# A transformer block on one core: halves of the attention output copied and added by GpSimd, q and k projected earlier

## The reference

```
def attention(x):                       # 16 heads of 64, batch 2, T = 1024
    q, k, v = x @ Wq, x @ Wk, x @ Wv
    logits = (q @ k^T + causal + position bias) / 64
    return softmax(logits) @ v @ Wo + bo
def moe(x):                             # one shared expert, 8 routed, top 2
    h = gelu(x @ Wfc + bfc) @ Wproj + bproj      # for each expert
    return shared + sum(gate_e * h_e)
x = x + norm(attention(norm(x)))
x = x + norm(moe(norm(x)))
```

## Time and profile before

| | |
|---|---|
| median of 3 runs | 946.14 us (944.57 to 946.49) |
| the profiled execution | 943.02 us, span 941.2 us |
| busy share of the span | TensorE 83%, VectorE 74%, ScalarE 67%, GpSimd 40% |
| TensorE's mean granted clock | 0.958 |
| attention, heads 0 to 15 | about 51 to 691 us |
| one turn of the loop (323.4 to 399.4 us) | 76.0 us, TensorE busy 66.9, VectorE 56.9, ScalarE 56.5, GpSimd 30.6 |

### The profile page before, as it was taken

The page is one execution under the profiler, slowest core; times in us unless marked ns, Lnnn a source line. Parts: engine busy times, 40 slices in busy tenths (PEclk is TensorE's granted clock), DMA queues, the critical chain, the costliest instruction groups (busy, mean ns, idle before and its releaser), DMA issues.

```text
span 941.2 us, 17424 instructions
## 1 busy us (share of the span) xinstructions
PE 784.5 (83%) x4244; PEld 640.4 (68%) x4244; DVE 700.9 (74%) x1564; ACT 632.4 (67%) x1404; POOL 377.5 (40%) x419
## 2 busy tenths in 40 slices
PE   3757799889888889879988988898657999999993
PEld 2546677668677778767767777777436777777772
DVE  5455587678778677858777867876658888889886
ACT  3356677767767776867777777786346677777763
POOL 1448544334435244324433433441231244444422
PEclk9998899999999999999999999999967999999997
DMA  7752433343344334433334334432100311111101
GB/s 249 264 170 64 96 74 79 81 95 84 68 95 99 76 67 90 95 79 73 81 90 97 69 79 102 84 72 63 56 23 1 115 68 67 67 67 67 45 1 45
DMA packets 61691, 79.01 MB, mean 84 GB/s; under 512 B 37312, under 2 KB 46656, under 8 KB 58304
## 3 DMA queue, kind: packets, MB, share of 16 engines
q1 hardware_dynamic: 61344, 77.84, 32.4%
q10 hardware_dynamic: 288, 0.59, 0.3%
HBM read 35.22 MB, written 9.63 MB: 48 GB/s over the span
## 4 chain that ended last, share of the span: by engine, by line
PE 47%; issue 15%; DVE 13%; DMA 10%; POOL 8%; ACT 4%; SPq 2%; DVEq 1%; POOLq 0%; ACTq 0%
PE out_ps L1298 11%; PE trans_ps L1280 8%; PE score_ps L1256 7%; DMA k_hl<-k_hl 5%; PE shared_ps L1312 3%; DMA inv_scratch<-normed 3%; PE score_ps L1168 2%; PE trans_ps L1168 2%; PE score_ps L1170 2%; PE score_ps L1169 2%; PE trans_ps L1169 2%; PE trans_ps L1170 2%; DVE pT_lo L949 2%; DVE pT_lo L1055 2%; POOL k_hl L544 2%
## 5 line engine op out<-in xcount | busy, mean ns | idle before, releaser
L936 DVE CUSTOM_DVE_ANT_0 score_ps<-score_ps,bias 128x128 f32<-128x128 f32 (+7 forms) x256 | 195.0, 762 | 117.7 <-PE score_ps L1256 96.1
L755 ACT ACTIVATE pT_hi<-trans_ps 128x512 fp32r<-128x512 f32 (+3 forms) x384 | 185.4, 483 | 124.6 <-PE trans_ps L1280 115.3
L1256 PE MATMUL score_ps<-k_hl,q_hl 128*128 128x512 f32 (+2 forms) x768 | 192.0, 360 | 40.9 <-DMA k_hl<-k_hl 32.3
L1280 PE MATMUL trans_ps<-ident,probs 128*128 128x128 f32 x1152 | 195.8, 282 | 35.0 <-DVE pT_lo L949 32.7
L949 DVE TENSOR_TENSOR pT_lo<-trans_ps,pT_hi 128x512 fp32r<-128x512 f32 (+3 forms) x384 | 204.2, 553 | 27.6 <-ACT pT_hi L755 25.7
L730 ACT ACTIVATE probs<-score_ps,row_min 128x128 f32<-128x128 f32 (+7 forms) x256 | 187.9, 734 | 35.2 <-DVE row_min L936 33.5
L1280 PEld LDWEIGHTS trans_ps<-ident,probs 128*128 128x128 f32 x1152 | 139.2, 144 | 74.0 <-DVE pT_lo L949 44.3
L1256 PEld LDWEIGHTS score_ps<-k_hl,q_hl 128*128 128x128 f32 x768 | 134.3, 191 | 71.4 <-ACT probs L730 26.8
L1298 PE MATMUL out_ps<-pT_hi,v_hl 128*128 128x512 f32 (+2 forms) x384 | 152.4, 401 | 17.9 <-DVE o_pair L967 17.9
L1055 DVE TENSOR_TENSOR pT_lo<-probs,pT_hi 128x512 fp32r<-128x512 f32 x144 | 133.7, 956 | 24.8 <-ACT pT_hi L824 14.3
L831 ACT ACTIVATE probs<-score_ps,layer_bias_T 128x512 f32<-128x512 f32 x144 | 98.5, 686 | 56.2 <-PE score_ps L1170 53.5
(11 more groups left out here) (127 smaller groups left out, 1249.2 us busy)
## 6 DMA issues: line engine op xcount, KB each, us to landing
q_hl<-k_hl SPq DMA_DIRECT2D x64, 256.0 KB, 3.3
k_hl<-k_hl SPq DMA_DIRECT2D x32, 512.0 KB, 4.3
v_scratch<-probs SPq DMA_DIRECT2D x16, 512.0 KB, 4.0
v_raw<-v_scratch SPq DMA_DIRECT2D x32, 256.0 KB, 3.9
inv_all<-inv_scratch SPq DMA_DIRECT2D x64, 128.0 KB, 3.1
bias_all<-gate_scratch SPq DMA_DIRECT2D x8, 1024.0 KB, 4.5
v_raw<-in_Wfc SPq DMA_DIRECT2D x8, 256.0 KB, 4.8
bias<-in_Wproj SPq DMA_DIRECT2D x8, 256.0 KB, 5.2
```

The source lines that it names most:

```text
L755: act.activation(pT_hi[c][:, CH * g:CH * g + m, q * P:(q + 1) * P], trans_ps[k % 2][:, 0:m * P].rearrange("p (m q) -> p m q", q=P), ACT.Co ...
L936: dve.tensor_tensor_reduce(out=ps, in0=ps, in1=bias_b[b][:, T - n:T], scale=1.0, scalar=3e38, op0=ALU.add, op1=ALU.min, accum_out=row_min[ ...
L1256: last = pe.matmul(scores_of(i)[:, at:end], q, k_hl[b][:, part, at:end], start=part == 0, stop=part == 1)
L1280: last = pe.transpose(trans_ps[k % 2][:, o:o + P], probs[s % 4][:, j * P:(j + 1) * P], ident[:])
```

## The change

The halves of `out_ps` leave the bank at once: ScalarE copies one as before, VectorE copies the other into a tile of its own (`keep_half`, in the slot in which the products end, behind `split_lo`), and GpSimd adds the two for a whole pair of heads at the head of `normalise_pair`. The next products wait for both copies. q and k of a head are projected in slots 2 and 3 of the block that lies fourteen slots before their use; `split_qk` stands at the first slot of the block before the use, and `split_wqk` at the head's slot 0 (in head 0, slot 1). `project_out` of the second chunk moves one slot on, which makes the tail one slot longer. SP issues `place_k` ahead of `load_inv` and `place_q` ahead of `store_inv`. `inv_row` gets memory of its own, the kept halves take that of `normed`, the router's small tiles that of `inv_all`.

```
-    WO = [12, 15]
-    SUM = [10, 14]
+    WO = [12, 16]
+    NORM = [10, 14]
-    QK = [0, 1]
+    QK = [2, 3]
-    QK_SLOT = {QK[0]: (0, 1, 0), QK[1]: (0, 1, 1), QB + QK[0]: (1, 0, 0), QB + QK[1]: (1, 0, 1)}
+    QK_SLOT = {QB * b + QK[half]: (1, b, half) for b in range(B) for half in range(NC)}
+    FIRST_QK = {0: (0, 1, 0), 1: (0, 1, 1)}
...
 SP, iteration
                 place_q(h, 1)
                 if not first:
                     store_inv(h - 1, 1, 1)
+                place_k(h, 1)
+                if not first:
                     load_inv(h - 1, 1, 1, m, not odd)
-                place_k(h, 1)
...
                 load_inv(h, 0, 0, m, odd)
+                if not last:
+                    place_q(h + 1, 0)
                 store_inv(h, 0, 1)
                 if not last:
-                    place_q(h + 1, 0)
+                    place_k(h + 1, 0)
                 load_inv(h, 0, 1, m, odd)
-                if not last:
-                    place_k(h + 1, 0)
...
 GpSimd
             def split_wqk(h):
+                if not (isinstance(h, int) and h < 2):
+                    pool.wait_ge(qk_psum, h * (2 * B))
...
             def normalise_pair(m, b, c):
+                n, u = (m - 1) * (B * NC) + b * NC + c, (m * 2 - 1) * (B * NC) + b * NC + c
+                pair = o_pair[b][c][:]
+                pool.wait_ge(o_copied, u + 1)
+                pool.sem_inc(pool_passed, 1)
+                pool.wait_ge(o_kept, u + 1)
+                pool.sem_inc(pool_passed, 1)
+                pool.tensor_tensor(pair, pair, kept[b][c], ALU.add).then_inc(o_added, 1)
                 pool.wait_ge(inv_loaded[b][c], m * 32)
                 pool.sem_inc(pool_passed, 1)
-                pool.wait_ge(o_summed, (m * 2 - 1) * (B * NC) + b * NC + c + 1)
+                pool.wait_ge(o_added, n + 1)
                 pool.sem_inc(pool_passed, 1)
-                pool.tensor_tensor(o_pair[b][c][:], o_pair[b][c][:], inv_all[b][c][:], ALU.mult).then_inc(o_ready, 1)
+                pool.tensor_tensor(pair, pair, inv_all[b][c][:], ALU.mult).then_inc(o_ready, 1)
             def slot(h, s, carried, last, m, odd):
-                for _, _, b, c in own_and_carried(SUM_SLOT, s, h, odd):
+                if s == 0 and carried and not last:
+                    split_wqk(h + 1)
+                if s == 0:
+                    for half in range(NC):
+                        split_qk(h, 1, half)
+                if s == 1 and not carried:
+                    pool.wait_ge(qk_psum, 2 * B)
+                    split_wqk(1)
+                if s == QB and not last:
+                    for half in range(NC):
+                        split_qk(h + 1, 0, half)
+                for _, _, b, c in own_and_carried(NORM_SLOT, s, h, odd):
                     normalise_pair(m, b, c)
-                if s in QK_SLOT:
-                    nxt, b, half = QK_SLOT[s]
-                    if not (nxt and last):
-                        split_qk(h + nxt, b, half)
...
                 if s == 5:
-                    pool.wait_ge(qk_psum, h * (2 * B) + 2 * B)
-                    if not last:
-                        split_wqk(h + 1)
...
 ScalarE, copy_other
-                if not odd and (b, c) == (0, 0) and not (isinstance(h, int) and h == 0):
-                    act.wait_ge(wo_psum, m * (B * NC))
+                if not odd and b == 0 and not (isinstance(h, int) and h == 0):
+                    act.wait_ge(wo_psum, (m - 1) * (B * NC) + (NC if c == 0 else B * NC))
...
 VectorE
-            def sum_halves(h, b, c, odd):
-
-                dve.wait_ge(o_copied, h * (B * NC) + b * NC + c + 1)
-                own_half = o_pair[b][c][half_of(odd), :]
+            def keep_half(h, b, c, j0, j1, m, odd):
+
+                if j1 < CH * (c + 1):
+                    return
+                if not odd and (b, c) == (0, 0) and not (isinstance(h, int) and h == 0):
+                    dve.wait_ge(o_ready, m * (B * NC))
+                    dve.sem_inc(dve_passed, 1)
+                dve.wait_ge(oT_psum, h * (B * NC) + b * NC + c + 1)
                 dve.sem_inc(dve_passed, 1)
-                dve.tensor_tensor(own_half, out_ps[half_of(odd), :], own_half, ALU.add).then_inc(o_summed, 1)
+                dve.tensor_copy(kept[b][c][half_of(odd), :], out_ps[half_of(odd), :]).then_inc(o_kept, 1)
...
             def slot(h, s, carried, last, m, odd):
                 row_minimum(h, s)
-                for n, before, b, c in own_and_carried(SUM_SLOT, s, h):
-                    sum_halves(n, b, c, odd != before)
                 if s >= LAG_DVE:
                     split_lo(h, s - LAG_DVE)
                 elif carried:
                     split_lo(h - 1, s - LAG_DVE + S)
+                for n, before, *part in own_and_carried(PV_SLOT, s, h):
+                    keep_half(n, *part, m, odd != before)
...
 TensorE, values
-                        pe.wait_ge(o_summed, u)
+                        pe.wait_ge(o_copied, u)
+                        pe.wait_ge(o_kept, u)
```

More of the change, by code:

```diff
@@ L90, in transformer_block, with qk_at, shared_uses @@
             WO_SLOT[QB * _b + WO[_c]] = (_b, _c)
-    QK_SLOT = {QK[0]: (0, 1, 0), QK[1]: (0, 1, 1), QB + QK[0]: (1, 0, 0), QB + QK[1]: (1, 0, 1)}
+    QK_SLOT = {QB * b + QK[half]: (1, b, half) for b in range(B) for half in range(NC)}
+    FIRST_QK = {0: (0, 1, 0), 1: (0, 1, 1)}
+    def qk_at(h, s, last):
+        first = FIRST_QK if isinstance(h, int) and h == 0 else {}
+        return [] if last else [(h + n, b, half) for n, b, half in ([first[s]] if s in first else [])
+                                + ([QK_SLOT[s]] if s in QK_SLOT else [])]
     TAIL = max(WO_SLOT) + 1
-    def shared_uses(odd):
-        wo = [(t % S, "wo", 0, b, c) for t, (b, c) in WO_SLOT.items() if (t < S) == odd]
-        uses = sorted([(t, "qk", n, b, half) for t, (n, b, half) in QK_SLOT.items()] + wo)
+    def shared_uses(odd, first=False):
+        wo = [(t % S, "wo", 0, b, c) for t, (b, c) in WO_SLOT.items() if (t < S) == odd and not first]
+        uses = sorted([(t, "qk", n, b, half) for t, (n, b, half) in QK_SLOT.items()] + wo
+                      + [(t, "qk", n, b, half) for t, (n, b, half) in FIRST_QK.items() if first])
         assert len({u[0] for u in uses}) == len(uses)
@@ L784, in slot @@
                 exp(h, s)
-                if s in QK_SLOT:
-                    nxt, b, half = QK_SLOT[s]
-                    if not (nxt and last):
-                        evacuate_qk(h + nxt, b, half)
+                for part in qk_at(h, s, last):
+                    evacuate_qk(*part)
             def iteration(h, m, odd):
@@ L1222, in wait_shared @@
             def wait_shared(h, s, last, m, odd):
-                uses = [u for u in shared_uses(odd) if u[0] < s and not (last and u[2] > 0)
+                uses = [u for u in shared_uses(odd, isinstance(h, int) and h == 0) if u[0] < s and not (last and u[2] > 0)
                         and not (isinstance(h, int) and h == 0 and u[1] == "wo")]
@@ L1324, in fillers @@
                     pieces.append(lambda b=b, c=c: project_out(m, b, c, 2, CH))
-                if s in QK_SLOT:
-                    nxt, b, half = QK_SLOT[s]
-                    if not (nxt and last):
-                        pieces.append(lambda: (wait_shared(h, s, last, m, odd), project_qk(h + nxt, b, half)))
+                for part in qk_at(h, s, last):
+                    pieces.append(lambda part=part: (wait_shared(h, s, last, m, odd), project_qk(*part)))
                 return pieces
```

46 lines of the change are left out of this document (24 added, 22 removed).

## The result

The changed kernel takes 956.79 us (median of 5 runs, 951.58 to 958.46) where the kernel before took 946.14 (5 runs, 944.52 to 950.72): a ratio of 1.0099, 95% interval 1.0064 to 1.0135. The forecast was 944.7. The profiled execution of the changed kernel took 951.58 us, with a span of 949.6; its own median lies 5.2 above that, as the median before lay 3.1 above its profile.

A forecast was written before the change was run, and what follows sets the result against it. No engine was full; TensorE's waits were taken as the bound. Steady -3.5, start -0.5 and tail +2.6 sum to -1.4, so 941.6 from the profiled 943.02; the median lying 3.1 higher gave 944.7 us, range 925 to 957.

The forecast's parts named there:

- I take 12.3 us as gone: Second blocks of odd heads: TensorE's waits for late k, 1.76 us each, disappear because k is projected earlier.
- the wait before slot 3: TensorE's wait for `sum_halves` to free the bank: it goes, 0.48 us in each of 30 blocks.
- what the moves expose: New TensorE waits: 0.7 in slot 1 (odd heads), 0.3 to 0.6 in slot 2, 0.45 in slot 3.
- Rival 1: Loop blocks: the exposed waits don't come, so gains stand bare: 910 us, or 927 with half of them; chance 0.26.
- rival 2: Slot 3's chain of projection, exp, eviction, projection: each block takes 0.3 us more, 953 us; chance 0.24.
- start and tail: Outside the steady part: start -0.5 us, with an 11 us wait in head 0's slot 2; tail +2.6 us.
- the last head: Last head's two blocks, within the steady sum: -1.2 us.
- Odd head, first block: Block at the loop's turn, from slot 1's transposes: 5.05 us before, 6.0 less 0.43 after, so +0.5.
- I put the change of their number at nothing: TensorE's clock dips, 1.4 us each: no change counted; three more, +4.2 us, only as a bound.
- after 6.0: Turn's block, from slot 1's transposes: 6.0 us after the change, before taking off 0.43; 5.05 before it.
- Rival 3: Start and clock: the start costs its upper bound, +4.5, and dips come at each turn, +4.2: 952 us; chance 0.06.
- rival 4: k is still late, so only the bank gains and 12.3 us comes back: 957 us; chance 0.03.

The follow-up runs named there:

- q later: The changed kernel, with SP waiting for the minimum of the head's slot 1 before the second batch's q copies: 947.38 us, ratio 0.9984.
- the late copies: The kernel before, with two extra copies of wqk per loop turn, issued by SP only after the head's second row minimum: 953.35 us, ratio 1.0021.
- moves alone: The changed kernel with VectorE's `sum_halves` back instead of the bank part: 958.51 us, ratio 1.0111; with q's copies delayed as well, 950.55 us, ratio 0.9976.
- the filled kernel: The kernel with both edits, GpSimd's last additions ahead of the tail's roots, plus 12 unused TensorE products at each turn: 932.55 us, ratio 0.9781.
- both edits: The changed kernel with SP's wait before q's copies and the first chunk's `keep_half` one slot later, behind `row_minimum`: 939.69 us, ratio 0.9911.

## Why the prediction failed, point by point

**Right: k and the bank.** "I take 12.3 us as gone" and the wait before slot 3: 0.8 and 1.1 us are left of 22.1 and 17.9. `keep_half` took 684 ns for 0.69.

**Right: what the moves expose, outside the turn.** Waits for the split in slots 1 and 2, and for the eviction between the projections: 10.6 us over 23, 0.46 each, for the 0.45 worked out. The three blocks came to -1.1, +0.25 and +0.22 for -1.3, +0.2 and +0.2. Rival 1 (no exposed waits) is out; rival 2 is too, since its extra 0.3 on the slot-3 chain did not come. The experiment with `keep_half` behind the minimum shows that this chain was real and avoidable: 8.4 us.

**Right: start and tail.** +0.45 for -0.5; the 11 us wait in slot 2 of head 0, k of (1, 0) at 94.6 for 94.9, the second wait until 103.6 for 103.2. Tail +2.3 for +2.6, with the last wait at 10.85 for 11.5. That the start agrees within 1 us is in part luck: the same code of head 0 reaches its slot 6 at 73.5 us here and at 77.0 in the profile of "q later", with more time at the lower clock.

**Missed, and a gain: the last head.** It projects nothing, since the next head doesn't exist. Its two blocks fell by 1.1 and 2.9 where I had 1.2 for both: 2.8 better. Some 1.25 of it is the clock: the profile before has a dip in the last block (20.43 us), and the three kernels with the same order and no dip there take 19.2.

**Wrong: the steps for the turn's block.** "Odd head, first block: [...] +0.5" and "I put the change of their number at nothing" (the clock dips). Six turns came to +11.9 for +3.0, which is 8.9 of the error. The other three kinds of block and roundings give 2.4 more, the first turn 0.7, the last head takes 2.8 back: 9.2 in all, from -3.5 to +5.7. Besides the dips the text had another term at nothing: the "after 6.0" of this block leaves VectorE's stall behind the jump as long as it was, although q's copies now run beside it. That these copies lengthen it is shown; how the rest of the 8.9 parts is an estimate.

*The clock.* In the two profiled executions the dips became more and longer: 20.5 us more at the turns, from 10.2 to 30.7. The price is to be had twice. Filling the stand took 23.9 us of low clock and 6.4 us of time away, 0.27 for one; in the kernel before the turns at clock 1.00 (20.1, 18.88 and 19.22) and those with a dip (20.85, 21.27 and 20.11) are 1.3 apart for 3.4, or 0.39. So by estimate the dips cost 5.5 to 8.0 in this pair. The text had named three more of them as a bound at +4.2, on the ground that "TensorE will stand 0.7 longer at each turn". It stood 1.2 longer (mean 3.46 for 2.28), 0.7 for the projection and 0.5 for VectorE's longer first stall, and every turn had a dip. The step should have asked what happens to a kernel that already loses its clock at half of its turns when the stand grows: the projections moved away were what kept TensorE busy there. Rival 3 had this at 0.06.

How much of it is the change's stays open. The profile before was that kernel's fastest execution (943.02 us, clock 0.958); the 61 executions measured beside the experiments have 0.942 to 0.956. The kernel before with the late copies has none of the change's moves, a stand of 2.70 us, a first stall of 3.74, and yet dips at all six turns and 30.7 us of low clock. The changed kernel's executions have a mean clock of 0.945; with q's copies later it is 0.950, the same as the kernel before on that chip. So that filling the stand takes dips and time away is shown, that the moved projections bring more dips than the kernel before usually has is not.

*The copies of q in the fetch.* The moved `place_q` was checked for what it is queued behind on SP, and for when q is needed. It was not checked for what its transfer meets. It now starts at 252.06, while VectorE stands and TensorE and ScalarE wait for it. The two kernels with and without SP's wait differ by 0.67 per turn, 4.0 us in all, some 0.9 to 1.3 of it by the clock: 3 remain. With the dips that makes 8.5 to 11 for the 8.9. The turn's own term then comes out at about the 0.5 forecast, or less; the runs don't part these better.

Over all executions the copies weigh more than in this pair. The forecast is 0.9985 of the first median before; the changed kernel has 1.0099, and with one wait ahead of q's copies 0.9984. By the ratios the copies are the whole error. That the rest then lands so close is luck as well: the last head's gain and the clock at the turns were not in the sum.

That copies lengthen the stall is shown both ways: taken away in two pairs of kernels (changed, and moves alone), put into the kernel before, and put there later. That what they put off is a transfer of instructions the traces show by its times: the second packet comes 1.3 us later on the mean, and VectorE's second stall is 1.3 us longer (1.95 for 0.67). That the packet is VectorE's is inferred from the fixed 1.9 us between them; why a copy holds it up is not shown. The Trainium skill (Runtime: NRT & Kernel Launch, Instruction fetch mechanics) says that a taken branch to a target outside the two resident pages forces a transfer of that page before execution goes on; the trace agrees as far as the stalls of 3.9 and 2 us and the packets ahead of their ends go.

The median, +10.6, is 2 us more than the difference of the two profiles (+8.6). Four of the changed kernel's five other executions show a mean clock of 0.941 to 0.946 for the profiled one's 0.948, so more dips are likely in them; the fifth took 955.77 us at 0.950, so dips aren't all of it. No trace shows more.

The measured 956.79 lies 0.2 inside the range of 925 to 957, and that is luck: its upper end was rival 4, a late k, and k was not late. Two slips of the text change nothing in the forecast: rival 3 adds up to 953.4 and not 952, and of the "three times" that TensorE stands in rows 2 the text and the rows have two.

## What to carry to other kernels

A transfer that is moved needs three questions, not two: what it is queued behind, when it is needed, and what is in flight beside it, the instruction fetch at a loop's turn above all; one wait on a row minimum took 9 us off. Work moved away from a place where an engine already stands takes its cover with it: look at the granted clock there first, over several executions, as a dip can come and go from one to the next. A new operation goes behind the instruction that another engine waits for, not ahead of it: the bank part is worth little (1.7 us by the medians) in one place and 6 to 11 one slot later, with q's copies out of the way.

## What the hardware did that I had not expected

- Two copies issued while VectorE stands behind the loop's jump lengthen its second stall from 0.65 us to 2 or 3; the same copies 7 us later don't. The second packet of the instruction queue comes 4.6 us behind the first instead of 2.7.
- Twelve useless products in each odd head of the loop (seven times, six of them behind a jump, 2.9 us each) took 6.4 us off the median and the 23.9 us of low clock between 118 and 644 us.
- The kernel before itself moved from 946 to 953 us between chips. Its executions on one chip ran from 946.06 to 957.32 us; those of the filled kernel, which has no dips in the loop, from 931.04 to 933.96 (four runs). The missing dips don't explain this narrowness: the kernel with both edits has a dip at each turn and ran from 939.33 to 940.78 (five runs).
